# Shared expert of a Mixture-of-Experts layer: one 128-wide tail group for gate and up, one 128-row tail for down, router products in pairs

## Chip, cores and metric

The kernel runs on one core of a Trainium2 chip. The metric is device time in microseconds (us) of one execution; several executions are timed and the median is given. PE is the engine that multiplies matrices (TensorE), DVE is VectorE, ACT is ScalarE, POOL is GpSimd, and SP issues most DMAs. Each engine works through its own instructions in order; semaphores tie the engines to one another.

## Reference

The whole kernel computes two transformer layers with attention and feed-forward parts. The change is in the shared expert and the router of the first feed-forward part, over T = 2048 tokens of width 512 with IS = 704 hidden columns:

```python
scores = softmax(x @ gate_w.T)                 # router: 16 experts
topk_w, topk_i = top_k(scores, 4)              # then sorted into per-expert slots
...
shared = silu(x @ sw_gate) * (x @ sw_up) @ sw_down   # (512x704), (512x704), (704x512)
y = routed_experts(x, topk_w, topk_i) + shared
```

`x` is layer-normalised here; the router's choices say which rows the 16 experts of the following stage gather.

## Kernel before

The stage is the function `ffn0_front_stage`. It runs from about 1062 us to 1303 us of the span, between the attention stage and the stage of the 16 experts. Instructions stand on each engine in the order in which the code issues them; nothing reorders them.

**Tiles.** The 2048 tokens are taken in B = 4 batches of L = 512. The 704 hidden columns are cut by `IT` into five groups of 128 and a sixth of 64 (`NI` = 6). Each f32 product is made of three matmuls (`mm3`, lines 120 to 122): every operand is split into a high part (ending in h) and a remainder (ending in l), and hi x lo, lo x hi and hi x hi are summed.

**PE.** For each batch b and group t, `gate_up(b, t)` computes the gate into bank `GB` and the up product into bank `UB`: 2 sides x 4 slices of the width (`KD` = 4) x 3 = 24 matmuls of 512 columns. Banks alternate by t % 2, so it first waits for `mid_done` of the group two before. After the six groups come four `down(b, i)`, one for each 128 tokens: 6 hidden pieces x 3 = 18 matmuls into `DN`; the sixth piece has 64 rows. `down` waits for `mid_lo` of each group (only i = 0) and, since `DN` has two banks, for `x_done` of the result two before. Batch 0 has more on PE: the transposes of the gate weights (`R`, line 1119), the turns (`turn`, line 1061) of the normalised rows of tokens 512 to 2047, which batches 1 to 3 read, and the router's products (`logits(i)`, line 1068: for each 128 tokens 4 matmuls of only 16 columns). Batch 1 has `ranks`, batch 2 four `collect`s (line 1112).

**ACT and DVE.** For each group ACT makes `sil` (silu of the gate), DVE multiplies it with the up product to `mid`, ACT makes the high half `midh`, DVE the remainder `midl`, on which `down` waits. DVE also adds each `down` result to the residual `x` (`add(n)`, line 1243, which gives `x_done`), splits the next batch's rows (`split_x`, after ACT's half), normalises rows in batch 0 (`norm_sums`, `norm_rows`), and carries the router: `route_centre` after batch 0's groups (it waits for `lg_ready`, all 16 token tiles' products), then ACT's exponentials, `route_probabilities`, in batch 1 `route_compare`, `route_mask`, `route_weights`, `route_positions`, `route_slots`, `route_choice`, in batch 2 four pairs of `route_partition(j)` and `route_rows(j)`, which feed the `collect`s.

**Weights.** `sw_gate` and `sw_up` are loaded during the last slots of the attention stage into free columns of `xT`; ACT and DVE split them into `gh`, `gl`, `uh`, `ul` at the start of the stage. `sw_down` is loaded into `rawd` and split into `dh`, `dl` within batch 0.

Of the kernel before, what the change touches and what calls it, by code (L numbers as in the profile page):

```python
# [24 lines left out]
F32 = mybir.dt.float32  # L25
# [99 lines left out]
def attention0_stage(nc, x, ident, tri, gates, xT, xh, xl, next_weights, next_loaded, xn_dram, x_in, ctx_in, wq_in, wk_in, wv_in, wo_in, wkc_in, wvc_in, qw_in, kw_in, g_xattn, g_ffn,  # L125
# [144 lines left out]
    with ExitStack() as ctx:  # L270
# [99 lines left out]
        with nc.Block() as block:  # L370

            @block.sync
            def _(sp):
# [74 lines left out]
                for s in range(SLOTS):  # L448
# [31 lines left out]
                    if s == NEXT_WEIGHTS_SLOT:  # L480

                        sp.wait_ge(xlo_ready, s + 4)
                        for j, src in enumerate(next_weights):
                            for k in range(KD):
                                sp.dma_start(xT[:, k, L + j * IS:L + (j + 1) * IS], src[k * P:(k + 1) * P]).then_inc(next_loaded[j][k], 16)
# [440 lines left out]
def ffn0_front_stage(nc, x, ident, tri, gates, xT, xh, xl, w_loaded, gate_in, consts, sd_in, ex_raw, ex_loaded, ex_weights,  # L926
# [10 lines left out]
    R0 = IT[0]  # L937
    NE = NT * E
# [5 lines left out]
    with ExitStack() as ctx:  # L944
        s = Scope(nc, ctx, "m")

        gh, gl, uh, ul = (ctx.enter_context(nc.sbuf_tensor(f"m_{q}", [P, KD, IS], F32R, side="right"))
                          for q in ("gh", "gl", "uh", "ul"))
# [45 lines left out]
        parts_taken = s.sem("parts_taken")  # L994
# [13 lines left out]
        def down_pieces():  # L1008
            return [(slice(0, R0), slice(0, 3)), (slice(0, R0), slice(3, NI - 1)), (slice(0, IT[-1]), slice(NI - 1, NI))]

        with nc.Block() as block:

            @block.sync
            def _(sp):
# [5 lines left out]
                sp.dma_start(rawd[0:IT[-1], NI - 1], sd_in[AT[-1]:IS]).then_inc(d_loaded, 16)  # L1020
# [33 lines left out]
            def _(pe):  # L1054
# [16 lines left out]

                def gate_up(b, t):
# [5 lines left out]
                    cs = slice(AT[t], AT[t] + IT[t])  # L1078
                    for j, (bank, wh, wl) in enumerate(((GB, gh, gl), (UB, uh, ul))):
# [37 lines left out]
                pe.wait_ge(gw_loaded, 16)  # L1117
                for k in range(KD):
                    last = pe.transpose(R[:, k * E:(k + 1) * E], gw[:, k * P:(k + 1) * P], ident[0:E, 0:E])
                last.then_inc(gw_turned, 1)  # L1120
# [27 lines left out]
            def _(act):  # L1148
# [12 lines left out]
                for j, hi in enumerate((gh, uh)):  # L1161
                    for k in range(KD):
                        act.wait_ge(w_loaded[j][k], 16)
                        act.activation(hi[:, k], raw[j][:, k], ACT.Copy).then_inc(w_hi, 1)
                for b in range(B):
                    for t in range(NI):
# [4 lines left out]
                        if n == 1:  # L1171
                            act.wait_ge(d_loaded, 32)
                            for q, r in down_pieces():
                                act.activation(dh[q, r], rawd[q, r], ACT.Copy).then_inc(d_hi, 1)
                        act.wait_ge(gu_full, n + 1)
# [4 lines left out]
                        act.activation(sil[0:IT[t], t % 2], GB[0:IT[t], t % 2], ACT.Silu).then_inc(silu_done, 1)  # L1180
# [3 lines left out]
                        act.activation(midh[0:IT[t], t], mid[0:IT[t], t % 2], ACT.Copy).then_inc(mid_hi, 1)  # L1184
# [10 lines left out]
            def _(ve):  # L1195
# [24 lines left out]
                def split_weight(j, k):  # L1220
                    hi, lo = ((gh, gl), (uh, ul))[j]
                    ve.wait_ge(w_hi, KD * j + k + 1)
                    ve.tensor_tensor(lo[:, k], raw[j][:, k], hi[:, k].bitcast(F32), ALU.subtract).then_inc(w_lo, 1)
# [10 lines left out]
                def group(b, t):  # L1234
                    n = NI * b + t
                    ve.wait_ge(silu_done, n + 1)
                    ve.tensor_tensor(mid[0:IT[t], t % 2], UB[0:IT[t], t % 2], sil[0:IT[t], t % 2], ALU.mult).then_inc(mid_done, 1)
                    ve.wait_ge(mid_hi, n + 1)
                    ve.tensor_tensor(midl[0:IT[t], t], mid[0:IT[t], t % 2], midh[0:IT[t], t].bitcast(F32), ALU.subtract).then_inc(mid_lo, 1)
# [110 lines left out]
                ve.tensor_copy(gwT[:], R[:, 0:KD * E].rearrange("p (k e) -> p k e", k=KD)).then_inc(gw_ready, 1)  # L1350
                for b in range(B):
                    for t in range(NI):
# [26 lines left out]
                        if b == 2:  # L1379
# [1221 lines left out]
```

## Time and profile before

| | |
|---|---|
| median of 3 timed executions | 1954.93 us (1954.01 to 1955.39) |
| profiled execution, from first to last instruction (span) | 1951.5 us |
| median less span (what lies around the span) | 3.4 us |
| mean granted TensorE clock over the span | 0.985 |
| PE busy over the span | 1834.0 us (94%) |
| DVE, ACT, POOL busy | 1096.8, 1036.9, 960.0 us |
| the shared expert's stage, first to last matmul | 1063.95 to 1301 us |

No own time of the profiled execution is given apart from its span, so the span and the 3.4 us around it stand for it. PE is busy nearly throughout, but a busy PE is only a matmul in flight: matmuls overlap, so what one costs in a row of matmuls is the distance between starts, not the duration in its row. "Granted clock" is 1.00 at 2.4 GHz and 0.50 at 1.2 GHz.

### The profile page before, as it was taken

Reading aid. Unit: us, or ns where it says so; the run is one execution under the profiler, and the core shown is the slowest. Engines: PE = TensorE matmul, PEld = TensorE weight load, DVE = VectorE, ACT = ScalarE, POOL = GpSimd, SP = SyncE. Lnnn points to the kernel's source line nnn. Section 1 sums busy time; section 2 is a strip of 40 time slices with the busy share of each in tenths; the row PEclk is TensorE's granted clock in tenths of the full one; section 3 lists DMA queues with packets and bytes.
Section 4 is the critical chain, followed back from the end, with each engine's and each line's share of the span. In section 5 each row is a group of like instructions: output and inputs, shape, how many; then the busy total and the mean of one; then the engine's idle time right before and its main releaser. Section 6 shows DMA issues by size and latency. Waiting matters only on the chain. (4 is left out here: it accounts for less than half of the span.)

```text
span 1951.5 us, 27620 instructions
## 1 busy us (share of the span) xinstructions
PE 1834.0 (94%) x9759; PEld 1317.1 (67%) x9796; DVE 1096.8 (56%) x2263; ACT 1036.9 (53%) x2248; POOL 960.0 (49%) x864
## 2 busy tenths in 40 slices
PE   7999999999999999999998999989999868869997
PEld 4667666776777666767765877769999646644443
DVE  5554444446445664456545648434343668768886
ACT  3655556655555545554544321126666367757775
POOL 5644455444654445544441100018888455657774
PEclk9999999999999999999999999999999989989999
DMA  7111112111111111011112100147889670000000
GB/s 240 56 51 47 42 35 57 55 32 51 34 40 34 49 55 46 18 34 50 51 65 79 66 22 22 44 136 218 229 235 259 186 162 1 1 1 23 23 17 28
DMA packets 112952, 141.18 MB, mean 72 GB/s; under 512 B 37408, under 2 KB 68128, under 8 KB 112624
## 3 DMA queue, kind: packets, MB, share of 16 engines
q1 hardware_dynamic: 105648, 122.63, 20.1%
q0 software_dynamic: 7168, 16.78, 4.2%
q8 instruction: 80, 1.31, 0.3%
q14 instruction: 56, 0.46, 0.1%
HBM read 104.78 MB, written 29.36 MB: 69 GB/s over the span
## 5 line engine op out<-in xcount | busy, mean ns | idle before, releaser
L750 POOL TENSOR_TENSOR a_xcl<-xT,a_xch 128x512 fp32r<-128x512 f32 x64 | 83.1, 1299 | 317.1 <-ACT a_xch L559 317.1
L909 PE MATMUL a_A<-a_pT,a_vf 128*128 128x512 f32 (+1 forms) x448 | 236.1, 608 | 1.4 <-ACT a_pT L575 1.2
L859 PE MATMUL a_S<-a_kT,a_qT 128*128 128x288 f32 (+3 forms) x640 | 208.8, 424 | 1.7 <-ACT a_pr_odd L565 1.7
L666 DVE TENSOR_REDUCE a_nmax<-a_S 128x1 f32<-128x192 f32 (+3 forms) x256 | 138.1, 551 | 80.5 <-PE a_S L860 79.2
L565 ACT ACTIVATE a_pr_odd<-a_S,a_nmax 128x320 f32<-128x320 f32 (+1 forms) x128 | 81.0, 634 | 152.4 <-DVE a_nmax L666 151.2
L120 PE MATMUL a_A<-a_wlo,a_xch 128*128 128x512 f32 x256 | 151.7, 592 | 2.6 <-DVE a_qT L662 2.6
L575 ACT ACTIVATE a_pT<-a_TR 128x512 f32<-128x512 f32 (+1 forms) x224 | 132.3, 591 | 35.5 <-PE a_TR L899 34.7
L859 PEld LDWEIGHTS a_S<-a_kT,a_qT 128*128 128x128 f32 x640 | 114.7, 189 | 49.6 <-issue 26.8
L1513 POOL TENSOR_TENSOR e_wlo<-expert_raw,e_whi 128x1408 fp32r<-128x1408 f32 x31 | 100.4, 3238 | 67.2 <-ACT e_whi L1685 65.1
L565 ACT ACTIVATE a_pr_even<-a_S,a_nmax 128x192 f32<-128x192 f32 (+1 forms) x128 | 67.1, 526 | 124.8 <-DVE a_nmax L666 124.7
L2429 PE MATMUL f_HH<-w12T,f_f_xqT 128*128 128x512 bf16 x496 | 117.7, 383 | 7.3 <-DVE f_h L2285 4.3
L706 DVE TENSOR_TENSOR a_otl<-a_A,a_oth 128x512 fp32r<-128x512 f32 x64 | 44.2, 691 | 137.8 <-ACT a_oth L579 137.8
L120 PE MATMUL a_A<-a_wlo,a_oth 128*128 128x512 f32 x256 | 111.1, 434 | 6.5 <-DVE a_otl L706 6.4
L120 PE MATMUL e_GUP<-e_xgl,e_whi 128*128 128x256 f32 (+1 forms) x384 | 110.4, 287 | 4.3 <-DVE e_xgl L1741 2.7
L121 PE MATMUL e_GUP<-e_xgh,e_wlo 128*128 128x256 f32 (+1 forms) x384 | 108.6, 283 | 0.0
L122 PE MATMUL e_GUP<-e_xgh,e_whi 128*128 128x256 f32 (+1 forms) x384 | 108.3, 282 | 0.0
L2064 POOL TENSOR_TENSOR f_hg<-f_h,g 128x512 f32<-128x512 f32 x64 | 81.6, 1275 | 52.6 <-DVE f_h L2285 52.6
L691 DVE RECIPROCAL a_rec<-a_rs 128x1 f32<-128x1 f32 x256 | 41.2, 161 | 111.1 <-ACT a_pr_odd L565 60.7
L122 PE MATMUL a_A<-a_whi,a_oth 128*128 128x512 f32 x256 | 101.1, 395 | 0.0
L121 PE MATMUL a_A<-a_whi,a_otl 128*128 128x512 f32 x256 | 100.7, 393 | 0.0
L122 PE MATMUL a_A<-a_whi,a_xch 128*128 128x512 f32 x256 | 100.7, 393 | 0.0
L121 PE MATMUL a_A<-a_whi,a_xcl 128*128 128x512 f32 x256 | 100.7, 393 | 0.0
(393 smaller groups left out, 5178.9 us busy)
## 6 DMA issues: line engine op xcount, KB each, us to landing
a_pw<-in_L_ffn_w_dram SPq DMA_DIRECT2D x96, 256.0 KB, 2.8
expert_raw<-in_L_ffn_w_gate_dram SPq DMA_DIRECT2D x16, 704.0 KB
expert_raw<-in_L_ffn_w_up_dram SPq DMA_DIRECT2D x16, 704.0 KB
expert_raw<-in_L_ffn_w_down_dram SPq DMA_DIRECT2D x16, 512.0 KB
tern<-a_tern SPq DMA_DIRECT2D x48, 128.0 KB, 1.8
x_res<-in_x_dram SPq DMA_DIRECT2D x4, 1024.0 KB, 9.3
a_raw<-in_L_xattn_wq_dram SPq DMA_DIRECT2D x4, 1024.0 KB, 5.5
a_raw<-in_L_xattn_wo_dram SPq DMA_DIRECT2D x4, 1024.0 KB, 5.4
```

The costliest lines, as they stand in the source:

```text
L120: pe.matmul(out, lhs_hi, rhs_lo, start=first, stop=False)
L121: pe.matmul(out, lhs_lo, rhs_hi, start=False, stop=False)
L122: return pe.matmul(out, lhs_hi, rhs_hi, start=False, stop=last)
L565: act.activation(pr[s % 2][:, i, 0:keys(s)], pair(s, i), ACT.Exp, bias=nmax[:, s % 2, i:i + 1], accum_out=rs[:, s % 2, i:i + 1]).then_inc( ...
L575: act.activation(pT[0:rows(i), i % 2], TR[0:rows(i), TR_USE["P", t, i][0]], ACT.Copy).then_inc(pT_ready, 1)
L666: ve.tensor_reduce(nmax[:, s % 2, i:i + 1], pair(s, i), AX.X, ALU.max, negate=True).then_inc(s_max, 1)
L750: pool.tensor_tensor(xcl[:, t % 2], xT[:, :, tok(t)], xch[:, t % 2].bitcast(F32), ALU.subtract).then_inc(xlo_ready, 1)
L859: pe.matmul(bank[:, lo:hi], qT[:, t % 2, hq], kT[:, par(t), lo:hi], start=True, stop=hi < nk)
L909: last = pe.matmul(A[:, A_USE["V", t, 0][0]], vf[r, par(t), i], pT[r, i % 2], start=i == 0, stop=i == nkt - 1)
L1513: pool.tensor_tensor(wlo[e % 2][q, cs], raw[q, e % 2, cs], whi[e % 2][q, cs].bitcast(F32), ALU.subtract).then_inc(gu_lo, 1)
L2064: pool.tensor_tensor(hg[:, u, part(n)], h[:, u, part(n)], g3[:, part(n)], ALU.mult).then_inc(hg_ready, 1)
L2429: last = pe.matmul(HH[pair_of(s, n)][j][:], f_xqT[:, u, j * KD + k], w12T[j][:, k, part(n)], start=k == 0, stop=k == KD - 1)
```

## Change

**Tail of gate and up.** The four weight tiles become two, `guh` and `gul`, of 2 x 704 columns: gate in its order, then up with its last 64 columns first. So the last 64 columns of gate and of up lie side by side, and the sixth group is one chain of 12 matmuls with 128 weight columns into `GB`, gate in partitions 0 to 63, up in 64 to 127 (`UP`). SP loads each of the four slices of `sw_up` in two pieces (4 more DMAs) so that they land in that order.

**Tail of down.** The last 64 rows are stacked to 128: `dl[0:64]` holds the remainder and `dl[64:128]` the high half (one more DMA, one more ACT copy, `d_copied`); `midh` holds the high half twice (one more ACT copy per batch, `tail_hi`), `midl` zeros and the remainder (one DVE memset at the start, `clear_ready`). The last piece is then two matmuls of 128 rows and not three of 64.

**Router.** The gate weights are turned after the first gate chain and not before it. The products of the first four token tiles come in two pairs, after groups 0 and 1 of batch 0, and those of the last pair after `down(0, 0)`; `down(0, 0)` and `down(0, 1)` get a wait for the copies of the turned rows, which shared `DN` with them. In batch 2 the last `route_partition` and `route_rows` move from group 5 to behind the first `add`.

```diff
@@ attention0_stage, SP
-                                sp.dma_start(xT[:, k, L + j * IS:L + (j + 1) * IS], src[k * P:(k + 1) * P]).then_inc(next_loaded[j][k], 16)
+                                at = L + j * IS
+                                for lo, hi in pieces:
+                                    sp.dma_start(xT[:, k, at:at + hi - lo], src[k * P:(k + 1) * P, lo:hi]).then_inc(next_loaded[j][k], 16)
+                                    at += hi - lo
...
@@ ffn0_front_stage, SP
-                sp.dma_start(rawd[0:IT[-1], NI - 1], sd_in[AT[-1]:IS]).then_inc(d_loaded, 16)
+                for rows in (slice(0, TAIL), UP):
+                    sp.dma_start(rawd[rows, LAST], sd_in[AT[LAST]:IS]).then_inc(d_loaded, 16)
@@ PE, gate_up
+                    if t == LAST:
+                        cs = slice(AT[t], AT[t] + P)
                         for k in range(KD):
-                            if n == 0:
-                                pe.wait_ge(w_lo, j * KD + k + 1)
-                            last = mm3(pe, bank[0:IT[t], t % 2], wh[:, k, cs], wl[:, k, cs], xh[:, k], xl[:, k], k == 0, k == KD - 1)
+                            last = mm3(pe, GB[:, t % 2], guh[:, k, cs], gul[:, k, cs], xh[:, k], xl[:, k], k == 0, k == KD - 1)
+                    else:
...
+                            if n == 0 and j == 0:
+                                turn_gates()
@@ PE, down
+                    else:
+                        pe.wait_ge(copied, NT - BT - 1 + n)
...
+                        if i == 0 and k == LAST:
+                            pe.wait_ge(tail_hi, b + 1)
...
-                        last = mm3(pe, DN[:, i % 2], midh[0:IT[k], k, tok], midl[0:IT[k], k, tok], dh[0:IT[k], k], dl[0:IT[k], k],
-                                   k == 0, k == NI - 1)
-                    last.then_inc(dn_full, 1)
+                        if k < LAST:
+                            mm3(pe, DN[:, i % 2], midh[:, k, tok], midl[:, k, tok], dh[:, k], dl[:, k], k == 0, False)
+                    pe.matmul(DN[:, i % 2], midl[:, LAST, tok], dl[:, LAST], start=False, stop=False)
+                    pe.matmul(DN[:, i % 2], midh[:, LAST, tok], dl[:, LAST], start=False, stop=True).then_inc(dn_full, 1)
@@ PE, order of the stage
                         if (b, t) == (0, 0):
                             pe.wait_ge(gw_ready, 1)
-                            for i in range(BT):
+                        if b == 0 and t < 2:
+                            for i in (2 * t, 2 * t + 1):
                                 logits(i)
...
-                        for i in (*late(NI - 2), *late(NI - 1)):
+                        for i in late(NI - 2):
                             logits(i)
...
                         down(b, i)
+                        if (b, i) == (0, 0):
+                            for r in late(NI - 1):
+                                logits(r)
@@ ACT
+                        if t == LAST:
+                            act.activation(midh[0:TAIL, t], mid[r, t % 2], ACT.Copy).then_inc(tail_hi, 1)
@@ DVE
+                ve.memset(midl[0:TAIL, LAST].bitcast(F32), 0.0).then_inc(clear_ready, 1)
...
-                            if t == 5:
-                                route_partition(3)
-                                route_rows(3)
...
                         add(BT * b + i)
+                        if (b, i) == (2, 0):
+                            route_partition(3)
+                            route_rows(3)
```

On PE, at the end of batch 0's groups, the order before is (m_DN<-ident_f,xg are turns, m_LG are router products with four matmuls to a tile, m_DN<-m_dl,m_midh opens a piece of `down`):

```order
L1061 MATMUL m_DN<-ident_f,xg 128x128 x8
L1068 MATMUL m_LG<-m_gwT,xT 128x16 x8
L1061 MATMUL m_DN<-ident_f,xg 128x128 x8
L1068 MATMUL m_LG<-m_gwT,xT 128x16 x16
L120 MATMUL m_DN<-m_dl,m_midh 128x512
```

The same place now, from the last products ahead of `down(0, 0)`; the row "..." leaves out four pieces like the one shown:

```order
L1073 MATMUL m_DN<-ident_f,xg 128x128 x8
L1080 MATMUL m_LG<-m_gwT,xT 128x16 x8
L120 MATMUL m_DN<-m_dl,m_midh 128x512
L121 MATMUL m_DN<-m_dh,m_midl 128x512
L122 MATMUL m_DN<-m_dh,m_midh 128x512
...
L1129 MATMUL m_DN<-m_dl,m_midl 128x512
L1130 MATMUL m_DN<-m_dl,m_midh 128x512
L1080 MATMUL m_LG<-m_gwT,xT 128x16 x8
L120 MATMUL m_DN<-m_dl,m_midh 128x512
```

Eight of the last sixteen products moved behind a whole `down`, whose sixth piece is now the two rows of lines 1129 and 1130.

On DVE, at the end of batch 2's groups, the order before is (xg<-m_numbers,m_at_part is `route_partition`, m_at_expert and xT are `route_rows`, xl is `split_x`, x_res is `add`):

```order
L1239 TENSOR_TENSOR m_midl<-m_mid,m_midh 64x512
L1320 TENSOR_TENSOR xg<-m_numbers,m_at_part 128x2048
L1324 TENSOR_TENSOR m_at_expert<-m_numbers,m_at_half 128x512
L1328 TENSOR_TENSOR xT<-m_at_expert,m_parts 128x1280 x2
L1232 TENSOR_TENSOR xl<-xT,xh 128x2048
L1243 SCALAR_TENSOR_TENSOR x_res<-m_DN,gates,x_res 128x512 x4
```

And now:

```order
L1275 TENSOR_TENSOR m_midl<-m_mid,m_midh 64x512
L1268 TENSOR_TENSOR xl<-xT,xh 128x2048
L1279 SCALAR_TENSOR_TENSOR x_res<-m_DN,gates,x_res 128x512
L1356 TENSOR_TENSOR xg<-m_numbers,m_at_part 128x2048
L1360 TENSOR_TENSOR m_at_expert<-m_numbers,m_at_half 128x512
L1364 TENSOR_TENSOR xT<-m_at_expert,m_parts 128x1280 x2
L1279 SCALAR_TENSOR_TENSOR x_res<-m_DN,gates,x_res 128x512 x3
```

The split of batch 3's rows and the first `add` now stand ahead of the last router tables.

## Rows read from the trace of the kernel before

**Rows 1.** Busy time by stretch: busy us and instructions per engine, granted clock, DMA share

```profile
1161.50:1191.80 30.30, 29.94 (x137) 21.30 (x135) 26.64 (x53) 5.49 (x7) 0.00 (x0) 1.00 0.06 22
...
1250.40:1283.30 32.90, 32.90 (x146) 25.86 (x146) 9.21 (x20) 6.15 (x10) 4.09 (x4) 1.00 0.14 41
1283.30:1301.30 18.00, 17.98 (x73) 12.75 (x71) 3.61 (x5) 1.23 (x2) 0.00 (x0) 1.00 0.86 285
```

**Rows 2.** Timeline of PE, batch 3: groups 4 and 5 begin, first `down` begins

```profile
1272.33 0.39 PE L120 MATMUL m_GB<-xl,m_gh 128*128 128x512 f32 x1
...
1277.77 0.40 PE L120 MATMUL m_GB<-xl,m_gh 128*64 128x512 f32 x1
...
1283.29 0.39 PE L120 MATMUL m_DN<-m_dl,m_midh 128*128 128x512 f32 x1
```

**Rows 3.** Timeline of PE, batch 3: third and fourth `down` begin

```profile
1292.18 0.50 PE L120 MATMUL m_DN<-m_dl,m_midh 128*128 128x512 f32 x1
...
1296.70 0.50 PE L120 MATMUL m_DN<-m_dl,m_midh 128*128 128x512 f32 x1
```

**Rows 4.** Busy time by stretch, with the granted clock ahead of the last two columns

```profile
1075.10:1078.50 3.40, 3.40 (x10) 2.64 (x10) 2.68 (x8) 0.41 (x1) 0.58 (x2) 0.52 0.05 16
...
1088.50:1091.00 2.50, 2.50 (x25) 2.50 (x23) 2.41 (x3) 1.63 (x4) 0.00 (x0) 1.00 0.00 0
1091.00:1092.20 1.20, 1.20 (x7) 1.01 (x7) 1.06 (x4) 0.00 (x0) 0.10 (x1) 1.00 0.00 0
...
1238.80:1242.20 3.40, 3.40 (x9) 2.65 (x10) 0.58 (x1) 0.00 (x0) 0.00 (x0) 0.54 0.41 154
```

**Rows 5.** Timeline of PE, batch 0: router products, group 1, first and third `down`

```profile
1071.48 3.64 PE L1068 MATMUL m_LG<-m_gwT,xT 128*128 128x16 f32 x32
1074.97 0.56 PE L120 MATMUL m_GB<-xl,m_gh 128*128 128x512 f32 x1
...
1116.41 3.94 PE L1068 MATMUL m_LG<-m_gwT,xT 128*128 128x16 f32 x32
1120.19 0.77 PE L120 MATMUL m_DN<-m_dl,m_midh 128*128 128x512 f32 x1
...
1130.53 0.50 PE L120 MATMUL m_DN<-m_dl,m_midh 128*128 128x512 f32 x1
```

**Rows 6.** Timeline of DVE, end of batch 0: last normalised row, `split_x`, first `add`

```profile
1112.68 0.55 DVE L1218 TENSOR_SCALAR xg<-x_res,m_mv,m_rstd 128x512 f32<-128x512 f32 x1 [0.44 <-POOL m_rstd L1044]
...
1125.35 2.29 DVE L1232 TENSOR_TENSOR xl<-xT,xh 128x2048 fp32r<-128x2048 f32 x1 [3.63 <-ACT xh L1159]
1127.56 0.75 DVE L1243 SCALAR_TENSOR_TENSOR x_res<-m_DN,gates,x_res 128x512 f32<-128x512 f32 x1
```

**Rows 7.** Timelines of DVE and PE, batch 1: group 3, second `add`, fourth `down`

```profile
1162.27 0.69 DVE L1237 TENSOR_TENSOR m_mid<-m_UB,m_sil 128x512 f32<-128x512 f32 x1 [1.81 <-ACT m_sil L1180]
...
1186.53 0.75 DVE L1243 SCALAR_TENSOR_TENSOR x_res<-m_DN,gates,x_res 128x512 f32<-128x512 f32 x1
...
1187.34 0.50 PE L120 MATMUL m_DN<-m_dl,m_midh 128*128 128x512 f32 x1 [0.36 <-DVE x_res L1243]
```

**Rows 8.** Timelines of DVE, ACT, PE, end of batch 2: group 5, tables, `collect`, `split_x`, third `down`

```profile
1227.82 0.68 DVE L1237 TENSOR_TENSOR m_mid<-m_UB,m_sil 64x512 f32<-64x512 f32 x1 [1.02 <-ACT m_sil L1180]
...
1229.08 1.90 ACT L1159 ACTIVATE xh<-xT 128x2048 fp32r<-128x2048 f32 x1
...
1229.82 2.28 DVE L1320 TENSOR_TENSOR xg<-m_numbers,m_at_part 128x2048 bf16<-128x2048 f32 x1
...
1231.40 1.28 PE L1112 MATMUL m_R<-xT,xg 128*128 128x160 bf16 x16
...
1235.77 2.29 DVE L1232 TENSOR_TENSOR xl<-xT,xh 128x2048 fp32r<-128x2048 f32 x1
...
1238.78 0.56 PE L120 MATMUL m_DN<-m_dl,m_midh 128*128 128x512 f32 x1 [1.75 <-DVE x_res L1243]
```

**Rows 9.** Chain of waits, 1064 to 1301 us: total us, times, longest

```profile
ACT m_sil L1180 <- PE m_UB L122: 112.5, 19, 25.2
```

More of the change, by code:

```diff
@@ L482, in _ @@
                         sp.wait_ge(xlo_ready, s + 4)
[L483 removed]
+                        for j, (src, pieces) in enumerate(zip(next_weights, ([(0, IS)], [(IS // P * P, IS), (0, IS // P * P)]))):
                             for k in range(KD):
[L485 removed]
+                                at = L + j * IS
+                                for lo, hi in pieces:
+                                    sp.dma_start(xT[:, k, at:at + hi - lo], src[k * P:(k + 1) * P, lo:hi]).then_inc(next_loaded[j][k], 16)
+                                    at += hi - lo
                     if s == TOTAL_SLOT:
@@ L937, in ffn0_front_stage @@
     R0 = IT[0]
+    LAST = NI - 1
+    TAIL = IT[LAST]
+    UP = slice(TAIL, 2 * TAIL)
     NE = NT * E
@@ L945, in ffn0_front_stage @@
         s = Scope(nc, ctx, "m")
-        gh, gl, uh, ul = (ctx.enter_context(nc.sbuf_tensor(f"m_{q}", [P, KD, IS], F32R, side="right"))
-                          for q in ("gh", "gl", "uh", "ul"))
+        guh, gul = (ctx.enter_context(nc.sbuf_tensor(f"m_{q}", [P, KD, 2 * IS], F32R, side="right")) for q in ("guh", "gul"))
         dh = s.sb("dh", [R0, NI, D], F32R)
@@ L1070, in logits, with turn_gates @@
                         last.then_inc(lg_ready, 1)
+                def turn_gates():
+                    pe.wait_ge(gw_loaded, 16)
+                    for k in range(KD):
+                        last = pe.transpose(R[:, k * E:(k + 1) * E], gw[:, k * P:(k + 1) * P], ident[0:E, 0:E])
+                    last.then_inc(gw_turned, 1)
                 def gate_up(b, t):
@@ L1115, in collect @@
                     last.then_inc(found_ready, 1)
[L1117 to L1120, printed above, removed]
                 for b in range(B):
@@ L1159, in split_x @@
                     act.activation(xh[:], xT[:, :, b * L:(b + 1) * L], ACT.Copy).then_inc(x_hi, 1)
-                for j, hi in enumerate((gh, uh)):
+                for j in range(2):
                     for k in range(KD):
-                        act.wait_ge(w_loaded[j][k], 16)
-                        act.activation(hi[:, k], raw[j][:, k], ACT.Copy).then_inc(w_hi, 1)
+                        act.wait_ge(w_loaded[j][k], 16 * (j + 1))
+                        act.activation(guh[:, k, side(j)], raw[j][:, k], ACT.Copy).then_inc(w_hi, 1)
                 for b in range(B):
@@ L1171, in _ @@
                         if n == 1:
-                            act.wait_ge(d_loaded, 32)
+                            act.wait_ge(d_loaded, 48)
                             for q, r in down_pieces():
                                 act.activation(dh[q, r], rawd[q, r], ACT.Copy).then_inc(d_hi, 1)
+                            act.activation(dl[UP, LAST], rawd[UP, LAST], ACT.Copy).then_inc(d_copied, 1)
                         act.wait_ge(gu_full, n + 1)
@@ L1179, in _ @@
                             act.wait_ge(parts_taken, 1)
-                        act.activation(sil[0:IT[t], t % 2], GB[0:IT[t], t % 2], ACT.Silu).then_inc(silu_done, 1)
+                        r = out_rows(t)
+                        act.activation(sil[r, t % 2], GB[0:IT[t], t % 2], ACT.Silu).then_inc(silu_done, 1)
                         if t == 0 and b > 0:
@@ L1183, in _ @@
                         act.wait_ge(mid_done, n + 1)
-                        act.activation(midh[0:IT[t], t], mid[0:IT[t], t % 2], ACT.Copy).then_inc(mid_hi, 1)
+                        act.activation(midh[r, t], mid[r, t % 2], ACT.Copy).then_inc(mid_hi, 1)
+                        if t == LAST:
+                            act.activation(midh[0:TAIL, t], mid[r, t % 2], ACT.Copy).then_inc(tail_hi, 1)
                     if b == 0:
@@ L1236, in group @@
                     ve.wait_ge(silu_done, n + 1)
-                    ve.tensor_tensor(mid[0:IT[t], t % 2], UB[0:IT[t], t % 2], sil[0:IT[t], t % 2], ALU.mult).then_inc(mid_done, 1)
+                    r, up = out_rows(t), GB if t == LAST else UB
+                    ve.tensor_tensor(mid[r, t % 2], up[r, t % 2], sil[r, t % 2], ALU.mult).then_inc(mid_done, 1)
                     ve.wait_ge(mid_hi, n + 1)
-                    ve.tensor_tensor(midl[0:IT[t], t], mid[0:IT[t], t % 2], midh[0:IT[t], t].bitcast(F32), ALU.subtract).then_inc(mid_lo, 1)
+                    ve.tensor_tensor(midl[r, t], mid[r, t % 2], midh[r, t].bitcast(F32), ALU.subtract).then_inc(mid_lo, 1)
                 def add(n):
```

21 lines of the change are left out of this document (15 added, 6 removed).

## Prediction

> **What bounds the kernel now.** The views were read in this order: the busy times by stretch, to see which engine fills which part of the stage; the timeline of PE, for what a matmul costs there; the timelines of DVE where PE waits for it; last the granted clock. PE is busy in nearly all of the stage. But DVE is busy for 26.64 of 30.30 us at the end of batch 1, and only for 9.21 of 32.90 us in batch 3 [rows 1]. So the reader is to see two kinds of stretch: in batch 3 a matmul less is time gained; at the end of batch 1 it may only be a longer wait for DVE. The fourth `down` of batch 1 starts 0.36 us late, on the second `add` [rows 7]: there both engines arrive together already. At the end of batch 2 the third `down` waits 1.75 us for an `add` [rows 8].
>
> The span is 1951.5 us and the median of the runs 1954.93 us; all terms are differences within the stage, taken from the span, and set against the median as they are.
>
> **The tail of gate and up.** A group of 24 matmuls with 128 weight columns takes 1277.77 - 1272.33 = 5.44 us, 0.227 us a matmul; the group with 64 columns takes 1283.29 - 1277.77 = 5.52 us [rows 2]. Half the columns save nothing. Twelve matmuls of the full width take 2.72 us, so each of the four batches has 2.8 us less on PE: 11.2 us.
>
> **The tail of down.** One `down` takes 1296.70 - 1292.18 = 4.52 us [rows 3], though 18 x 0.227 is 4.09: the piece of 64 rows costs 0.43 us more than its three matmuls. Seventeen matmuls, all of 128 rows, should take 17 x 0.227 = 3.86 us. That is 0.66 us less, 16 times: 10.5 us. If the 0.43 us hung on something other than the 64 rows, only 0.23 us would be left of it, 3.6 us in all; I take 10.5, since the only stretch of `down` at another spacing is that piece.
>
> **The clock in batch 0.** After the 32 products of 16 columns, 3.49 us from 1071.48 to 1074.97 [rows 5], PE runs at a granted clock of 0.52 for 3.4 us; after turns and 16 products, 2.5 us, it stays at 1.00 [rows 4]. So at the first place half of 3.4, 1.7 us, is given back by taking products in pairs. A pair costs 3.49 / 2 = 1.75 us. The products ahead of the first `down` lower the clock too: two `down` take 1130.53 - 1120.19 = 10.34 us and not 9.04, 1.3 us more [rows 5]. There the change leaves turns, a pair, turns, a pair, some 6 us without a wide matmul, so I keep 1.3 us.
>
> **Batch 0, and a new wait.** On PE group 5 ends 1.7 + 2.8 = 4.5 us earlier. The last rows that it turns are then late: their normalisation ends at 1113.23 [rows 6], and DVE is ahead there by only 1.2 us (1.7 less 0.5 for ACT's additional copy for `dl`, which stands before the silu that DVE follows). So the turns end at about 1112.6, the pair at 1114.4, and the first `down` starts there and not at 1120.19. It ends after 3.86 + 1.3 us at 1119.6, and the pair that was moved behind it at 1121.3. `route_centre` needs that pair. Behind it on DVE stand `split_x` and the first `add`: from the end of the products at 1120.19 to the end of that `add` at 1128.31 [rows 5, 6] are 8.1 us, which two `down` cover before. Now only one stands behind the products: PE is done with it at 1125.2, and the third `down` must wait for the `add` until 1129.4, 4.2 us. It starts 1.1 us earlier than at 1130.53. After 1.75 us of waiting in batch 2 PE ran at 0.54 for 3.4 us [rows 4, 8], so this wait costs a further 1.7 us; two shorter `down` give back 1.3. Batch 0 gains 0.7 us of the 7.1 that PE is relieved of. With no low clock at either place it gains 3.7.
>
> **Batch 1.** DVE works from group 3's `mid` at 1162.27 to the end of the second `add` at 1187.28 with no room: 25.0 us [rows 7]. The change takes nothing from that chain; ACT's second copy of `midh` may add 0.1 us ahead of its half of `split_x`. PE comes to the fourth `down` 2.8 + 3 x 0.66 = 4.8 us earlier and waits, in pieces: for `mask_ready`, for the last `mid_lo`, for the `add`s. What remains is the last `down`, 0.66 us, and the 0.36 us of before is not won. The last of the waits, about 2 us, may lower the clock: 0 or 1.7 us; I take 0.9, between the 0.36 us wait that did not and the 1.75 us one that did. Batch 1: -0.3 us.
>
> **Batch 2.** PE has 2.8 + 4 x 0.66 = 5.4 us less. The router tables that stood ahead of `split_x` and the first `add`, 1229.82 to 1235.77 [rows 8], now stand behind them, so the wait of 1.75 us and its 1.7 us of low clock go: 3.45 us. New waits: DVE stood still for only 1.02 us ahead of group 5's `mid` [rows 8], so the last `mid_lo` can come only about 1.0 us earlier, while PE reaches the sixth piece 2.9 us earlier and had about 0.5 us to spare: 1.4 us. And `collect(3)` needs the moved tables: from the last `mid_lo` they end after the rest of ACT's additional copy and its half of `split_x` (1.90), `split_x` (2.2), `add` (0.7) and the tables (5.95) [rows 8], some 10.4 us after PE starts on the sixth piece, where PE needs 0.45 + 1.28 + 2 x 3.86 = 9.4: 1.0 us. Batch 2: 5.4 + 3.45 - 1.4 - 1.0 = 6.4 us.
>
> **Batch 3.** DVE has room, and five pieces of the first `down` (3.4 us) cover silu, `mid`, both copies and `midl`, about 2.9 us. 2.8 + 4 x 0.66 = 5.4 us. The experts' loads are issued when the last group ends and keep the DMA engines busy for 0.86 of the 18 us behind it, 15.5 us [rows 1]; the four `down` still last 15.4 us and the first expert's half is needed first, so this end is not late.
>
> **Taken at nothing.** ACT's copies (five of 0.6 us): it stands idle for 112.5 us on the gate banks alone [rows 9]. The memset of 64 x 512 lies in DVE's work of batch 0, ahead of a `mid` that nobody needs for two groups. The five DMAs on SP: those of the weights are issued in the attention stage and used in this one, with only the last rows' stores behind them on SP, and that of the tail of `sw_down` has until ACT's copies in group 1. The turn of the gates moves behind the first chain, and the first matmul waits for the weights' split instead. Each would cost at most its own length, 0.3 to 3 us.
>
> **Sum.** 0.7 - 0.3 + 6.4 + 5.4 = 12.2 us. Some ten stretches of narrow work or waiting are left (eight pairs, some with turns, and the waits of 1.0 to 1.5 us). They resemble the place that kept the clock more than those that lost it [rows 4], and a fall costs 1.7 us; I take 0.7 of one, 1.2 us. The forecast is 1954.9 - 11.0 = 1943.9 us.
>
> The Trainium skill, page "TensorE: Matmul & The Clock Gate", section "HAM oscillation — how this bites in real kernels", tells of a loop whose waits drop the array to half rate again in every pass. The rows agree for the 1.75 us wait and not for the 0.36 us one; by it every new wait would count, which is the last rival below at 1962.6 us.
>
> **Rivals.**
> - The 0.43 us stays in each `down`: 6.9 us less, of which the waits in batches 0 and 1 hide some 2. 1948.8 us. For it: the last piece still takes its operands from other tiles than the rest. Against: in the groups the change from `GB` to `UB` and of the weight tiles costs nothing [rows 2].
> - PE's relief comes through whole, because DVE's chains shorten with PE: 11.2 + 10.5 + 1.7 + 3.45 = 26.9, 1928 us. Against it stands the 0.36 us wait [rows 7]: DVE is the later one already.
> - The change does little: the clock falls at five or more further places, 5 x 1.7 = 8.5 us of the 11. 1952.4 us. For it: two stretches of batch 0 lose the clock now. Against: the pair with turns kept 1.00 [rows 4].
> - Slower: the clock falls after all eight pairs and all six new waits. Without any fall the sum of 12.2 is 3.0 + 0.9 more, 16.1 us; 14 x 1.7 = 23.8 us takes that back: 1962.6 us. It decides from the tenth fall on. Against it: rows 4 and the 0.36 us wait.
>
> **Numbers.** The forecast 0.71, the tail that stays 0.12, the whole relief 0.05, little 0.08, slower 0.04. A difference of 0.2% (3.9 us) is about what a measurement of this kernel can tell from no change. Faster: 0.71 + 0.12 + 0.05 and a part of the fourth, 0.89; within 0.2%: 0.07; slower: 0.04. The upper end, 1950.7 us, is the forecast with four further falls of the clock or the tail that stays with one; the lower, 1938.8, is the sum with no fall at all. Beyond are the whole relief, the rest of the fourth and the last.
>
> **What would show it.** Right: the sixth group 2.7 us and each `down` 3.9 us; a wait of about 4 us ahead of batch 0's third `down`, on `add`; waits of 1 to 2 us ahead of `ranks`, the sixth piece and the fourth `down` of batch 1; no wait on `add` in batch 2; the clock at 1.00 after the first pair; batch 3 shorter by 5.4 us. Wrong: a `down` of 4.3 us, no wait after the moved pair, or a granted clock near 0.5 after most pairs.

## Result, and the profile after

The changed kernel takes 1943.65 us (median of 4, 1942.04 to 1946.50) against 1955.16 us (median of 4, 1954.01 to 1957.32): ratio 0.9946, 95% interval 0.9932 to 0.9961. The forecast was 1943.9 us. In a later set, five further runs of it gave 1947.98 us and 0.9965, interval 0.9951 to 0.9979 (e0 below). The change is faster both times; by how much is only known to some 3 us to either side. That the first median lies 0.25 us from the forecast is luck: the second lies 4 us from it.

Part of the scatter lies outside the stage. From the experts' first turn to the end of the span it is 1951.5 - 1303.52 = 648.0 us before and 1942.9 - 1296.21 = 646.7 us after, but 650.5 us in e0, which is the same program. The experiments are therefore also compared by the stage alone: from the start of the first gate matmul to the start of the experts' first turn (`e_TR`). PE's timeline of the kernel before, where batches 1, 2 and 3 and the experts begin (start, duration; its first gate matmul is at 1064.30):

```profile
1139.55 0.50 PE L120 MATMUL m_GB<-xl,m_gh 128*128 128x512 f32 x1
...
1191.85 0.50 PE L120 MATMUL m_GB<-xl,m_gh 128*128 128x512 f32 x1
...
1250.44 0.50 PE L120 MATMUL m_GB<-xl,m_gh 128*128 128x512 f32 x1
...
1303.52 0.72 PE L1552 MATMUL e_TR<-ident_f,xg 128*128 128x128 f32 x4 [2.24 <-PEq L100]
```

The same rows of the changed kernel, with those of batch 0 ahead (router products, first `down`, last pair, second, third and fourth `down`) and group 5 and the last two `down` of batch 3:

```profile
1064.30 0.80 PE L120 MATMUL m_GB<-xl,m_guh 128*128 128x512 f32 x1 [3.89 <-DVE m_gul L1258]
...
1073.00 1.85 PE L1080 MATMUL m_LG<-m_gwT,xT 128*128 128x16 f32 x16
1074.70 0.49 PE L120 MATMUL m_GB<-xl,m_guh 128*128 128x512 f32 x1
...
1114.59 3.43 PE L1080 MATMUL m_LG<-m_gwT,xT 128*128 128x16 f32 x16
1117.86 0.77 PE L120 MATMUL m_DN<-m_dl,m_midh 128*128 128x512 f32 x1
...
1123.34 1.85 PE L1080 MATMUL m_LG<-m_gwT,xT 128*128 128x16 f32 x16
1125.04 0.49 PE L120 MATMUL m_DN<-m_dl,m_midh 128*128 128x512 f32 x1
...
1133.20 0.79 PE L120 MATMUL m_DN<-m_dl,m_midh 128*128 128x512 f32 x1 [4.00 <-DVE x_res L1279]
...
1139.49 0.39 PE L120 MATMUL m_DN<-m_dl,m_midh 128*128 128x512 f32 x1
...
1143.35 0.39 PE L120 MATMUL m_GB<-xl,m_guh 128*128 128x512 f32 x1
...
1195.55 0.39 PE L120 MATMUL m_GB<-xl,m_guh 128*128 128x512 f32 x1
...
1248.45 0.39 PE L120 MATMUL m_GB<-xl,m_guh 128*128 128x512 f32 x1
...
1275.65 0.39 PE L120 MATMUL m_GB<-xl,m_guh 128*128 128x512 f32 x1
...
1278.37 0.39 PE L120 MATMUL m_DN<-m_dl,m_midh 128*128 128x512 f32 x1
...
1286.07 0.39 PE L120 MATMUL m_DN<-m_dl,m_midh 128*128 128x512 f32 x1
...
1289.93 0.39 PE L120 MATMUL m_DN<-m_dl,m_midh 128*128 128x512 f32 x1
...
1296.21 1.06 PE L1589 MATMUL e_TR<-ident_f,xg 128*128 128x128 f32 x8 [2.26 <-PEq L100]
```

From start to start, batch 0 takes 75.25 us before and 79.05 after, 3.8 us longer. Batch 1 takes 52.30 and 52.20, batch 2 58.59 and 52.90, batch 3 with the way to the experts 53.08 and 47.76. The gain of 7.3 us in the stage is all of batches 2 and 3. Group 5 takes 2.72 us where it took 5.52 [rows 2], and a `down` 3.86 us where it took 4.52 [rows 3].

PE's waits in the stage after (total us, times, longest; DVEq and PEq are the engines' own sequencers):

```profile
PE m_DN L120 <- DVE x_res L1279: 6.2, 3, 4.0
PE m_GB L120 <- DVE m_gul L1258: 3.9, 1, 3.9
PE m_DN L1129 <- DVE m_midl L1275: 2.6, 2, 1.3
...
PE m_R L1134 <- DVE m_mask_b L1310: 1.3, 1, 1.3
PE m_R L1144 <- DVEq L1367: 1.1, 1, 1.1
```

The three on `x_res` are the third `down` of batch 0 (4.0) and the third and fourth of batch 1 (0.5 and 1.7). DVE's timeline, with the last normalised row of batch 0 ahead, shows why the first is so long: the products end, the router's chain runs, and `split_x` and the first `add` stand behind it:

```profile
1113.36 0.55 DVE L1254 TENSOR_SCALAR xg<-x_res,m_mv,m_rstd 128x512 f32<-128x512 f32 x1 [0.44 <-POOL m_rstd L1056]
...
1125.22 0.42 DVE L1287 COPY m_lg<-m_LG 128x256 f32<-128x256 f32 x1 [6.85 <-PE m_LG L1080]
...
1130.19 2.29 DVE L1267 TENSOR_TENSOR xl<-xT,xh 128x2048 fp32r<-128x2048 f32 x1 [3.62 <-ACT xh L1191]
1132.40 0.75 DVE L1279 SCALAR_TENSOR_TENSOR x_res<-m_DN,gates,x_res 128x512 f32<-128x512 f32 x1
```

That is 8.1 us from the products' end to the end of the `add`, as before [rows 5, 6], but now with one `down` to cover it. Stretches of the changed kernel (busy us of PE, PEld, DVE, ACT, POOL, then the granted clock) show the half clock at the stage's start, around the first `down` and behind the 4.0 us wait, the full one around the first two pairs and behind the 1.7 us wait, and batch 3 [rows 1, 4]:

```profile
1064.30:1070.00 5.70, 5.70 (x15) 4.08 (x16) 5.55 (x7) 5.06 (x7) 0.00 (x0) 0.51 0.85 273
1073.00:1082.00 9.00, 9.00 (x58) 8.00 (x56) 6.12 (x17) 1.23 (x2) 2.11 (x3) 1.00 0.28 104
1114.60:1120.60 6.00, 6.00 (x24) 5.42 (x24) 2.49 (x3) 2.21 (x4) 0.00 (x0) 0.50 0.13 48
1131.60:1138.10 6.50, 4.90 (x12) 3.84 (x13) 3.30 (x6) 0.00 (x0) 0.00 (x0) 0.50 0.21 81
1190.00:1196.00 6.00, 4.44 (x19) 3.68 (x20) 5.83 (x16) 0.00 (x0) 0.00 (x0) 1.00 0.16 62
...
1278.30:1296.20 17.90, 15.64 (x70) 12.64 (x69) 4.65 (x7) 1.86 (x4) 0.00 (x0) 1.00 0.91 299
```

### The profile page after: what moved, and what is told of

Its sections match the earlier page's. It is cut to its first block and busy times, and to the rows that moved or that the text cites. A ratio compares the mean times of both kernels' runs of the same rounds, so it can differ in the third digit from the quotient of the medians.

```text
span 1942.9 us, 27508 instructions
## 1 busy us (share of the span) xinstructions
PE 1818.2 (94%) x9695; PEld 1314.9 (68%) x9732; DVE 1098.4 (57%) x2264; ACT 1039.7 (54%) x2253; POOL 958.4 (49%) x864
## 6 DMA issues: line engine op xcount, KB each, us to landing
expert_raw<-in_L_ffn_w_down_dram SPq DMA_DIRECT2D x16, 512.0 KB, 10.5
```

## Experiments

The theory after the result: the matmuls saved are worth their time only where DVE is not the later engine, and moving the last pair behind the first `down` cost batch 0 more than it gave. Rival: PE's relief comes through whole, and something unrelated took it in batch 0. All runs; each ratio is to the kernel before on the same chip, with an interval of 0.0009 to 0.0015 to either side:

| | stage: from, to, us | median us | ratio |
|---|---|---|---|
| before | 1064.30, 1303.52: 239.2 | 1955.16 | |
| changed | 1064.30, 1296.21: 231.9 | 1943.65 | 0.9946 |
| e0 changed again | 1062.01, 1295.51: 233.5 | 1947.98 | 0.9965 |
| e1 sixth group twice | 1064.72, 1300.97: 236.3 | 1948.84 | 0.9969 |
| e2 pair back | 1064.42, 1291.24: 226.8 | 1941.49 | 0.9932 |
| e3 wait filled | 1062.51, 1291.35: 228.8 | 1941.32 | 0.9933 |
| e4 split_x and add first | 1062.47, 1289.37: 226.9 | 1941.14 | 0.9933 |
| e5 tables back | 1063.52, 1299.82: 236.3 | 1951.02 | 0.9986 |
| e6 weights later | 1062.77, 1295.91: 233.1 | 1946.51 | 0.9965 |
| e7 combined | 1063.85, 1287.02: 223.2 | 1939.34 | 0.9921 |
| e8 three of 64 rows | 1062.12, 1299.32: 237.2 | 1950.71 | 0.9984 |
| e9 three of 128 rows | 1064.25, 1298.37: 234.1 | 1948.63 | 0.9975 |
| e10 gates first | 1064.49, 1297.24: 232.8 | 1949.07 | 0.9972 |
| e11 router spread | 1062.29, 1280.38: 218.1 | 1930.87 | 0.9886 |

In e10 and e11, as in the kernel before, the turn of the gates stands ahead of the stage so taken (0.53 us, 0.35 before); in the others it is within.

**e0, the changed kernel again.** 

> The changed kernel as it is, as the level for the other runs on this chip: ratio 0.9946 again, 1943 to 1945 us. In its trace: a wait of about 4 us ahead of the third down of batch 0, that down 6.3 us long, and waits of 1 to 2 us in batch 1.

All waits came again; the median was 4 us higher than the first. Of the stage's 1.6 us more, all lies behind the wait of the fourth `down` of batch 1. PE's timeline of e0: pieces there are 1.28 us apart, at half clock, and not 0.68:

```profile
1189.27 0.50 PE L120 MATMUL m_DN<-m_dl,m_midh 128*128 128x512 f32 x1 [1.78 <-DVE x_res L1279]
...
1191.02 0.63 PE L120 MATMUL m_DN<-m_dl,m_midh 128*128 128x512 f32 x1
...
1192.30 0.63 PE L120 MATMUL m_DN<-m_dl,m_midh 128*128 128x512 f32 x1
```

The same wait left the clock at 1.00 in the first trace, and in e1, e2, e3 and e5. It lowered it in e0, e4 and e10: three of eight.

**e1, the sixth group's matmuls made twice.**

```diff
-                        for k in range(KD):
-                            last = mm3(pe, GB[:, t % 2], ...)
+                        for bank in (UB, GB):
+                            for k in range(KD):
+                                last = mm3(pe, bank[:, t % 2], ...)
```

> The 12 matmuls of the sixth group are made twice (first into the other bank, where nobody reads them): PE has 12 x 0.227 = 2.7 us more in each batch, 10.9 us in all. Theory (DVE's chain decides in batches 1 and 2): batch 0 +2.5, batch 1 0 (the waits of 1.3, 1.3, 0.5 and 1.7 us shrink by as much), batch 2 +0.7 (the waits of 1.3 and 1.1 us shrink), batch 3 +2.7: 6 us slower than the changed kernel, 4 to 7.5. Rival (PE's relief comes through whole): 10.9 us slower, back to before or above.

Against the changed kernel's trace, batch 0 is 0.8 us longer, batch 1 0.0, batch 2 0.8, batch 3 2.7: 4.3 us for 10.9 us of matmuls (2.8 us against e0). Batches 1 to 3 came out as the theory has them, the rival is out. Batch 0 was expected at 2.5. With a later group 5 the last row was there when its turn came, and turns and products from group 5 to the first `down` took 5.8 us and not 7.7 (the last pair 2.3 and not 3.3). The half clock came later instead: the first `down` took 6.6 us and not 5.5, the third 5.3 and not 6.3. The medians differ by 0.9 us only, less than their scatter can tell.

**e2, e3, e4, the wait in batch 0.** In e2 PE takes all four last products ahead of `down(0, 0)`:

```diff
-                        for i in late(NI - 2):
+                        for i in (*late(NI - 2), *late(NI - 1)):
                             logits(i)
...
-                        if (b, i) == (0, 0):
-                            for r in late(NI - 1):
-                                logits(r)
```

> The last pair of router products stands ahead of the first down again, with the rest of the change kept. Theory (moving the pair behind one down cost more than it gave, by a wait of 4.0 us and the half clock behind it): the first down starts 2 to 3 us later, the wait ahead of the third down is under 0.5 us, that down takes 3.9 us and not 6.3; 4.5 to 7 us faster than the changed kernel, 1937 to 1940 us. Rival (the narrow products ahead of the first down cost as much as the wait): within 1.5 us of the changed kernel.

In e3 PE works through the wait:

```diff
+                        if (b, i) == (0, 1):
+                            for _ in range(18):
+                                pe.matmul(R[:], midh[:, 0, 0:P], dh[:, 0], start=True, stop=True)
```

> 18 matmuls of 512 columns (4.1 us) that nobody reads stand where PE waits 4.0 us ahead of the third down of batch 0; all else as in the changed kernel. Theory (the half clock of the third down follows from PE standing still): the third down starts at the same time and takes 3.9 us at a granted clock of 1.00, 2.4 us faster than the changed kernel. Rival (the half clock belongs to the narrow products two downs earlier, or falls in any case): the third down keeps 6.3 us, no gain.

In e4 the order changes on DVE and ACT alone:

```diff
+                        split_x(1)
                         act.wait_ge(copied, NT - BT)
                         act.wait_ge(centred, 1)
                         act.activation(flat(pm), flat(lg), ACT.Exp).then_inc(exp_done, 1)
-                    if b + 1 < B:
+                    elif b + 1 < B:
                         split_x(b + 1)
...
-                    if b == 0:
-                        route_centre()
                     if b + 1 < B:
                         split_x(b + 1)
                     for i in range(BT):
                         add(BT * b + i)
+                        if (b, i) == (0, 0):
+                            route_centre()
...
-                        if (b, i) == (0, 0):
+                        if (b, i) == (0, 1):
                             route_probabilities()
```

> On DVE split_x and the first add of batch 0 stand ahead of route_centre, and ACT makes its half of split_x ahead of the exponentials; PE's order is that of the changed kernel, with the pair behind the first down. Theory (the wait of 4.0 us is only the order on DVE: add and split_x stand behind a chain that starts from the last products): the third down starts at 1129.0 and not 1133.2, and at full clock, 2.4 us more: 6.5 us faster than the changed kernel, 5 to 7.5; later batches move as one, since DVE moves with them. Rival (DVE gives the time back in batch 1 or 2, where it is the later one): 2 us or less faster.

PE's timelines, third and fourth `down` of batch 0: first e3 (behind the 18 matmuls), then e4:

```profile
1130.63 0.50 PE L120 MATMUL m_DN<-m_dl,m_midh 128*128 128x512 f32 x1
...
1134.62 0.39 PE L120 MATMUL m_DN<-m_dl,m_midh 128*128 128x512 f32 x1
```

```profile
1127.18 0.39 PE L120 MATMUL m_DN<-m_dl,m_midh 128*128 128x512 f32 x1
...
1131.03 0.39 PE L120 MATMUL m_DN<-m_dl,m_midh 128*128 128x512 f32 x1
```

In e3 the third `down` takes 3.99 us and not 6.29, though PE gets no earlier `add`: in this pair of traces, the 2.3 us were the clock behind standing still. Its price is not the same each time: behind a 4.0 us wait the third `down` took 6.3 us in the first trace, e0 and e10, 5.3 in e1 and 5.4 in e5 and e6. In e4 there is no wait, and batch 0 lasts 72.4 us, 6.6 less than in the changed kernel (6.5 were expected), all of which is still there at the stage's end against e0, which shares e4's half clock in batch 1. So the pair can stay behind the first `down` if DVE's order is right. In e2, with DVE's order left as it was, the wait is gone too and batch 0 lasts 74.0 us, 5.1 less: the wait needs both, the moved pair and the chain ahead of `add`. The first `down` of e2 starts 3.4 us later, after 32 products at half clock, 6.6 us:

```profile
1114.77 6.78 PE L1080 MATMUL m_LG<-m_gwT,xT 128*128 128x16 f32 x31
1121.39 0.77 PE L120 MATMUL m_DN<-m_dl,m_midh 128*128 128x512 f32 x1
```

**e5, the last tables of batch 2 in group 5 again** (the change's own diff undone there). 

> The last route_partition and route_rows of batch 2 stand in group 5 again, ahead of split_x and the first add; the rest of the change is kept. Theory: the first add of batch 2 ends 5.9 us later, PE waits some 5 us ahead of the third down instead of 1.1 us ahead of collect, and runs at half clock behind it: 4 to 6.5 us slower than the changed kernel. Rival (batch 2 gains by fewer matmuls alone, the order on DVE gives nothing): within 1 us.

The stage is 4.4 us longer, 3.9 of them in batch 2. The wait was 3.3 us, not 5; the half clock behind it adds 1.7, and the 1.1 us wait of `collect` is gone:

```profile
1241.42 0.50 PE L120 MATMUL m_DN<-m_dl,m_midh 128*128 128x512 f32 x1 [3.31 <-DVE x_res L1279]
...
1243.15 0.63 PE L120 MATMUL m_DN<-m_dl,m_midh 128*128 128x512 f32 x1
```

The theory holds. Without this move 2.9 us of the stage's 7.3 are left, and a ratio of 0.9986.

**e6, DVE's router weights later in batch 1.**

```diff
-                            if t == 4:
-                                route_weights()
-                            if t == 5:
-                                route_positions()
...
-                        if b == 1:
+                        if (b, i) == (1, 1):
+                            route_weights()
+                            route_positions()
+                        if b == 1 and i > 0:
+                            route_choice(i - 1)
+                        if (b, i) == (1, BT - 1):
                             route_choice(i)
-                        if (b, i) == (1, BT - 1):
                             route_parts()
```

> In batch 1 route_weights and route_positions (3.8 us on DVE) stand behind the second add and not ahead of group 5's mid and split_x; each route_choice but the last comes one add later. Theory (DVE is the later one without a break from group 3 of batch 1 to the last tables of batch 2): the waits of 1.3, 0.5 and 1.7 us in batch 1 go, PE is 3.4 us earlier there, and batch 2 gives all but 0.3 to 1 us of it back in waits for tables and mid. Rival (batch 1 alone is short of DVE): 3 to 3.5 us faster than the changed kernel.

Batch 1 is 3.9 us shorter from its first `down` on, and batch 2 gives it back with 1.3 us more; the stage is 1.2 us longer than in the first trace. PE has a new wait in batch 2, on `mid`, and the one on `midl` is longer by 1.3 us:

```profile
PE m_DN L1129 <- DVE m_midl L1275: 2.5, 1, 2.5
PE m_GB L120 <- DVE m_mid L1273: 2.0, 1, 2.0
```

Behind the wait on `mid` the clock falls:

```profile
1203.00:1206.50 3.50, 3.48 (x10) 2.71 (x11) 2.77 (x2) 1.12 (x2) 0.00 (x0) 0.60 0.00 0
```

That group takes 7.2 us and not 5.4. Without these 1.8 us the move would, by this estimate, have kept some 0.5 us, within the 0.3 to 1 expected. DVE is the later engine from batch 1's group 3 to the last tables: shortening its chain in one place moves the wait.

**e7, these together, the last tables in batch 3.** Beside e4 and e6: `route_mask` reduces in three pieces, and `route_partition(3)`, `route_rows(3)`, `collect(3)`, `route_table` move to batch 3's groups 0, 2 and 3. 

> The orders of e4 and e6 together; the mask's reduction of 4.4 us is made in three pieces, two of them in groups 1 and 2 where DVE stands still 1.8 us per group; the last route_partition, route_rows, their collect and route_table move to batch 3, where DVE has room. Theory: 6.5 us in batch 0, 4.7 in batch 1 (waits of 1.3, 1.3, 0.5 and 1.7 us), 1.5 to 2.4 in batch 2, nothing lost in batch 3: 11 to 13 us faster than the changed kernel, 1931 to 1933 us. Rival (the relief ends in other waits, on ACT's or DVE's per-group work): 6 to 8 us.

8.7 us shorter than the first trace, 10.3 than e0; 11 to 13 was too much. Batch 2 kept waits on `mid` (1.7), tables (1.5) and `midl` (2.5).

**e8 and e9, the price of 64 rows.** e8 makes three matmuls of the lower 64 partitions in place of the last two, e9 makes the first of the two twice. 

> The last piece of each down is three matmuls of 64 rows instead of two of 128; the operands of all three lie in the lower 64 partitions, so the high part's products of the last 64 columns are left out of the sum. Theory (the piece of 64 rows costs 0.43 us beside its matmuls): a down of batch 3 takes 4.5 us again, 0.66 us more; of 10.5 us on PE some 6.8 come through, the rest lies in waits. Rival (the 0.43 us came from the other tiles of the operands, not from the rows): 4.1 us a down, some 2 us in all.

> The first of the two matmuls of the last piece is made twice, so three matmuls of 128 rows (the remainders' products of the last 64 columns count twice). Theory: a down of batch 3 takes 17 + 1 matmuls of 0.227 us, 4.09 us, 0.23 more than in the changed kernel; 3.6 us on PE, of which some 2 come through. Rival (a third matmul of the last piece costs 0.66 us whatever its rows): 4.5 us a down.

PE's timelines, second and third `down` of batch 3, e8 and then e9:

```profile
1283.45 0.50 PE L120 MATMUL m_DN<-m_dl,m_midh 128*128 128x512 f32 x1
...
1287.96 0.50 PE L120 MATMUL m_DN<-m_dl,m_midh 128*128 128x512 f32 x1
```

```profile
1283.70 0.39 PE L120 MATMUL m_DN<-m_dl,m_midh 128*128 128x512 f32 x1
...
1287.78 0.39 PE L120 MATMUL m_DN<-m_dl,m_midh 128*128 128x512 f32 x1
```

4.51 us with 64 rows, 4.08 with 128: the 0.43 us is the price of the 64-row piece. The kernel before, whose piece read other tiles, took 4.52 [rows 3]. In the stage, e8's 10.5 us cost 5.3 and e9's 3.6 cost 2.2.

**e10, the gates turned first again.**

```diff
-                            if n == 0 and j == 0:
-                                turn_gates()
...
+                turn_gates()
                 for b in range(B):
```

> The gate weights are turned ahead of the first gate chain again, with the rest of the change kept. Theory (the small matmuls ahead of the chain shorten the half clock behind the stage's first wait: in the kernel before it lasted 3.4 us from 1064.9 on, in the changed one until 1070): the first group takes 7.2 us with the turn outside it and not 8.3, its clock is back at 1.00 by 1068.5, and the stage is 1 to 1.5 us shorter. Rival (the longer half clock has another cause, such as the tiles of 1408 columns): the clock is back only at 1070, and the stage is as long as in the changed kernel or 0.3 us longer.

The half clock lasts until 1069.3, nearly as long as in the changed kernel, and not until 1068.2 as in the one before. From the attention's last matmul to the first products it is 12.3 us and not 12.6. The theory fails: with the order of before, the clock was already low at the turn (0.53 us where it took 0.35). The length of this half clock is not fixed by the order. In e3 and e6, where the turn stands behind the first chain as in the changed kernel, the first gate matmul took 0.50 us as in the kernel before, not 0.80, and the first group 7.9 us with the turn in it, not 8.7. PE's timeline of e3, first gate matmul and first products:

```profile
1062.51 0.50 PE L120 MATMUL m_GB<-xl,m_guh 128*128 128x512 f32 x1 [3.89 <-DVE m_gul L1261]
...
1070.37 1.85 PE L1080 MATMUL m_LG<-m_gwT,xT 128*128 128x16 f32 x16
```

So one trace of each kernel can't tell what the change did to it. What decides when the clock falls here stays open.

**e11, the router's work spread over batches 2 and 3.** On DVE:

```diff
                         if b == 2:
-                            if t in (0, 1, 3):
-                                route_partition((t + 1) // 2)
-                            if t in (0, 2, 4):
-                                route_rows(t // 2)
+                            if t < 2:
+                                route_choice(t + 2)
+                            if t == 2:
+                                route_parts()
+                                route_partition(0)
+                            if t == 3:
+                                route_rows(0)
+                        if b == 3:
+                            if t == 1:
+                                route_partition(3)
+                            if t in (0, 2):
+                                route_rows(2 + t // 2)
+                            if t == 4:
+                                route_table()
...
+                        if (b, i) in ((2, 0), (2, 2)):
+                            route_partition(1 + i // 2)
+                        if (b, i) == (2, 1):
+                            route_rows(1)
```

> The orders of e4 and e10; the mask's reduction in pieces and route_weights, route_positions behind the second add as in e7; the router's further work on DVE is spread so that no group of batch 2 has more than 3.7 us of it: route_choice(2) and (3) in groups 0 and 1 of batch 2, the first tables in groups 2 and 3, the others behind batch 2's adds and in batch 3, with their collects, and route_table in batch 3's group 4. Theory (e7's waits of 1.7 on mid, 1.5 on tables and 2.5 on mid_lo in batch 2 are DVE's queue): they go, 5.7 us beyond e7, and 1 us of the first group: the stage from the first gate chain to the experts' first matmul takes 217 to 218 us where the changed kernel takes 231.9, 1930 to 1934 us. Rival (the stage ends in another wait, or the gathers of the first experts' rows come late): 222 us or more, no better than e7.

1930.87 us (1929.10 to 1931.35), ratio 0.9886, interval 0.9871 to 0.9901; the stage takes 218.1 us. PE's waits from 1070 us to the experts:

```profile
PE e_TR L1596 <- PEq L100: 2.3, 1, 2.3
PE m_R L1142 <- DVEq L1365: 1.2, 1, 1.2
PE m_DN L1073 <- DVE xg L1252: 0.3, 1, 0.3
```

From 1118 us, within the first `down` of batch 0, to the experts it is at full clock:

```profile
1118.00:1282.00 164.00, 159.92 (x766) 131.70 (x764) 98.38 (x171) 32.46 (x46) 4.08 (x4) 1.00 0.17 59
```

This version beats both kernels: the stage is 21.1 us shorter than before, about as much as the 11.2 + 10.5 us of matmuls that the change took away. It isn't the same sum: the kernel before also had 1.75 us of wait and 1.6 of half clock in batch 2 to give back, and e11 still has the half clock at the stage's start and around the first `down` of batch 0. What each of e11's moves gave was not measured one by one.

## Why the prediction was right, and where it was not

The number was right in part by luck; the sum behind it was not quite. The sum was 11.0 us in the stage; the traces show 7.3 (5.7 in e0). The first median lay 11.5 us below the one before, e0's 6.1; the rest lies outside the stage, or in executions of which no trace is kept.

- **The tails.** Right in size: 2.72 us for group 5, 3.86 for a `down`; e8 and e9 show that the 0.43 us hung on the 64 rows.
- **Batch 0, +0.7 forecast, -3.8 measured.** The mechanism was right: a wait of 4.0 us (4.2 forecast) on `add`, from the same 8.1 us chain, with half clock behind it. The step that failed is the clock's length, and above all the first term, "1.7 us, is given back by taking products in pairs". The third `down` started 3.8 us later than forecast (1133.2, not 1129.4) and took 0.7 us more.
  - 2.0 us were lost when the turns ended (1114.6, forecast 1112.6). The clock did stay at 1.00 behind the first pair, and group 1 took 1.6 us less. But the half clock of the stage's start lasted until 1070, and the turn of the gates, taken at nothing, came into the chain: 8.70 us for the first group, 7.18 before. Of these 1.5 us some 1.2 are the half clock (an estimate: half of the 2.3 us by which it lasted longer, 5.6 against 3.3), the rest the turn. Group 1 began only 0.27 us earlier, group 2 only 0.11. DVE was not 1.2 us ahead but 0.7 behind: the last normalised row ended at 1113.9, and PE waited 0.3 us for it. e3 and e6 show that 0.8 us of the long first group come and go with the execution.
  - 1.5 us were the pair ahead of the first `down`, taken as 1.75 us: 3.27, because the clock was low from its first matmul on. 0.3 us was the first `down`, 5.5 us where 5.2 was forecast.
  - 0.7 us was the third `down`: taken with 1.7 us more, it had 2.4 more here, and 1.4 to 1.6 in e1, e5 and e6.
- **Batch 1, -0.3 forecast, +0.1 measured** (-1.5 in e0). Right: waits of 1.3, 1.3, 0.5 and 1.7 us took the relief, and the half fall of the clock (0.9 us) was a whole one (1.6) or none.
- **Batch 2, +6.4 forecast, +5.7 measured.** Right: the wait on `add` is gone, the new ones are 1.3 on `midl` (1.4 forecast) and 1.1 on the tables (1.0). e5 shows that the moved tables carry 3.9 us of it.
- **Batch 3, +5.4 forecast, +5.3 measured.**
- **The 0.7 of a further fall of the clock, -1.2.** In batches 2 and 3 it fell nowhere; the falls of batch 0 were longer instead.
- **The rivals.** Whole relief: out by e1. The tail that stays: out by e8. Clock at every new wait: of the waits of 1.7 to 1.8 us on `add` in batch 1 three in eight lowered it, those of 1.1 to 1.3 none. The Trainium skill, page "TensorE: Matmul & The Clock Gate", section "HAM oscillation — how this bites in real kernels", has a loop whose waits, some 3 to 5 us long, drop the clock in every pass. The 4.0 us wait did so in every trace that has it (first, e0, e1, e5, e6, e10), the shorter one in batch 1 only in some. The change does little (2.5 us less), or is slower: out by both measurements.

## What to carry to other kernels

A shorter chain of matmuls is worth what the engine behind it has in room, read stage by stage; where it has none, moving that engine's work to a stretch where it stands still (e11) gives more than the matmuls alone. Before moving a small product behind a large one, follow who waits for it, and what that engine has queued behind: here `add` stood behind a chain of 8 us. When two runs of one program differ by 4 us, compare the stage in the trace and not the medians, and allow for the clock even there: between executions of one order it moved the stage by 1.6 us in batch 1 and by 0.8 at the start.

## What was not expected of the hardware

A matmul piece of 64 rows among pieces of 128 costs 0.43 us beside its matmuls, with either choice of tiles that was tried (4.51 against 4.08 us for a `down` with as many matmuls). The Trainium skill, page "TensorEngine Tiling (Array Packing)", section "Tiling Modes", says that a change of the tiling mode drains the engine, and lists 64 rows as a mode of its own. e8 and e9 fit that, with 0.43 us for the way there and back; that a drain is what takes the time, no run shows by itself. A group with 64 weight columns cost only 0.08 us beside its matmuls, 5.52 us against 5.44 [rows 2].

A wait of 1.7 to 1.8 us lowered the granted clock in three of eight executions, at the same place. Length alone does not decide: a wait of 2.0 us on `mid` lowered it in e6, and the 2.5 us wait on `midl` left it at 1.00 in e6 and in e7. Every wait of 3.3 to 4.0 us ahead of a third `down` lowered it (first trace, e0, e1, e5, e6, e8, e9, e10). With 18 matmuls that nobody reads in place of the 4.0 us wait it stayed at 1.00, and the `down` behind them took 3.99 us, not 6.29.
